# First query chunk of a causal attention turned to keys down the partitions, and the row statistics of chunks three and four moved ahead

## What is computed

```
xn = layernorm(x)
x_norm = (xn - mu) / sqrt(var + EPS) * gamma + beta
q, k, v = x_norm @ qkv[:, :512], x_norm @ qkv[:, 512:1024], x_norm @ qkv[:, 1024:]
scores = where(causal, (q @ k.T) / sqrt(512), -inf)
attn = softmax(scores) @ v @ o_proj + xn
h = silu(xn @ w_gate) * (xn @ w_up)
ffn = (of every 4 neighbours of h the 2 largest in size, the others 0) @ w_down
out = x + attn + ffn
```

## Time and profile before

| | us |
|---|---|
| median of 3 runs | 803.7 (800.33 to 805.3) |
| the profiled execution, its own time | 802.02 |
| span of the profile | 800.2 |
| PE busy | 788.8 (99%), 3518 matmuls |
| DVE busy | 610.8 (76%) |
| ACT busy | 319.6 (40%) |
| POOL busy | 18.9 (2%) |
| mean granted PE clock | 0.994 |

### The profile page before, as it was taken

How to read it: one execution, slowest core, us unless ns; L and a number is a source line. 1 busy time by engine, 2 the same in 40 slices (tenths; PEclk the granted TensorE clock), 3 DMA queues, 4 the chain that set the end, 5 groups by cost and what they waited for, 6 DMA issues and landing times.

```text
span 800.2 us, 9296 instructions
## 1 busy us (share of the span) xinstructions
PE 788.8 (99%) x3518; PEld 651.7 (81%) x3518; DVE 610.8 (76%) x964; ACT 319.6 (40%) x514; POOL 18.9 (2%) x26
## 2 busy tenths in 40 slices
PE   9999979989999999999999999999999999999998
PEld 6888858878888888888888888888888888888887
DVE  7978497775824688779989889799559558559786
ACT  5423142124312354564636436364334334335441
POOL 2010110101000000000000000000000000000000
PEclk9999989999999999999999999999999999999999
DMA  9441501730022325587426435497467262261002
GB/s 325 174 169 44 185 0 61 255 106 1 27 79 79 109 102 220 174 325 280 185 73 266 188 79 210 180 348 291 154 214 262 102 235 92 95 236 54 0 1 106
DMA packets 31611, 121.74 MB, mean 152 GB/s; under 512 B 3088, under 2 KB 3664, under 8 KB 29136
## 3 DMA queue, kind: packets, MB, share of 16 engines
q1 hardware_dynamic: 30272, 119.00, 40.4%
q10 hardware_dynamic: 1296, 2.16, 0.8%
HBM read 77.07 MB, written 44.07 MB: 151 GB/s over the span
## 4 chain that ended last, share of the span: by engine, by line
PE 78%; DMA 2%; DVE 1%; issue 0%; ACT 0%; SPq 0%; DVEq 0%
PE bank L960 13%; PE bank L961 13%; PE bank L962 13%; PE bank L1040 7%; PE bank L1042 7%; PE bank L1041 7%; PE bank L701 5%; PE bank L699 5%; PE bank L700 5%; PE bank L840 2%; DMA spread<-row_stats 1%; DMA resid<-rows 0%; DMA row_stats<-rows_turned_t 0%; DVE xh_raw L1541 0%; DVE xh_raw L1543 0%
## 5 line engine op out<-in xcount | busy, mean ns | idle before, releaser
L960 PE MATMUL bank<-X_hi,wset 128*128 128x512 f32 x448 | 174.4, 389 | 0.0
L962 PE MATMUL bank<-X_hi,wset 128*128 128x512 f32 x448 | 174.3, 389 | 0.0
L961 PE MATMUL bank<-X_lo,wset 128*128 128x512 f32 x448 | 174.3, 389 | 0.0
L960 PEld LDWEIGHTS bank<-X_hi,wset 128*128 128x128 f32 x448 | 84.1, 188 | 17.6 <-issue 0.2
L962 PEld LDWEIGHTS bank<-X_hi,wset 128*128 128x128 f32 x448 | 84.1, 188 | 17.5
L961 PEld LDWEIGHTS bank<-X_lo,wset 128*128 128x128 f32 x448 | 84.1, 188 | 17.4
L1040 PE MATMUL bank<-dw,hs_hi 128*128 128x512 f32 x224 | 87.2, 389 | 0.0
L1042 PE MATMUL bank<-dw,hs_lo 128*128 128x512 f32 x224 | 87.1, 389 | 0.0
L1041 PE MATMUL bank<-dw,hs_hi 128*128 128x512 f32 x224 | 87.1, 389 | 0.0
L1674 DVE TENSOR_TENSOR acc<-bank,acc 128x512 f32<-128x512 f32 x59 | 40.1, 687 | 40.0 <-PE bank L1042 39.6
L699 PE MATMUL bank<-zg,xT 128*128 128x512 f32 (+2 forms) x132 | 49.8, 377 | 0.0
(11 more groups left out here) (259 smaller groups left out, 1441.7 us busy)
## 6 DMA issues: line engine op xcount, KB each, us to landing
w_operands<-wset SPq DMA_DIRECT2D x8, 3584.0 KB, 13.5
wset<-w_operands SPq DMA_DIRECT2D x8, 3584.0 KB, 12.5
wsum<-w_units SPq DMA_DIRECT2D x28, 256.0 KB, 3.8
dw_raw<-L_ffn_w_down SPq DMA_DIRECT2D x14, 512.0 KB, 5.4
xw<-L_attn_x SPq DMA_DIRECT2D x4, 1024.0 KB, 9.6
xt_raw<-x_t SPq DMA_DIRECT2D x8, 512.0 KB, 7.5
xn_t<-xt_raw SPq DMA_DIRECT2D x8, 512.0 KB, 2.8
acc<-resid SPq DMA_DIRECT2D x2, 2048.0 KB, 9.8
```

Source lines behind the costliest of these rows:

```text
L960: pe.matmul(dst[:], u[:, 0, :], x_hi, start=(first and kt == 0), stop=False, skip_group_check=True)
L961: pe.matmul(dst[:], u[:, 0, :], x_lo, start=False, stop=False, skip_group_check=True)
L962: last = pe.matmul(dst[:], u[:, 1, :], x_hi, start=False, stop=(kt == 1), skip_group_check=True)
```

## The change

`WIDE` becomes all four chunks. The code of the other way (`scores`, `exp`, `head`, `attend`, with their turns, masks and buffers) goes away. Chunk 0 gets four units, a maximum with one half instead of two (`largest`), three softmax parts and its own sums (`first_sums`). All stores and loads of rows go to SP's queue. `turn_rows` puts the turned statistics of chunks 2 and 3 in bank 2 of the score ring (`LENT_BANK`), lent between two units of chunk 1. The statistics of chunk 2 move into chunk 0's softmax, those of chunk 3 amid the units of chunk 1. The core of the diff:

```
-    exp = [("exp", n, 0) for n in range(NT)]
-    WIDE = (1, 2, 3)
-    OLD = TC * WIDE[0]
-    for i in range(OLD):
-        ...
-        steps.append(("head", i, 0))
...
+    WIDE = range(NCH)
...
+    u = unit[0]
+    steps += [v[0][0], *u[0:2], x_scale[1], u[2], row_turn[1], row_copy[1], row_store[1], row_spread[1], u[3], ("max_all", 0, 0), v[0][1], *stat[2][0:2]]
+    steps += softmax(0, {-1: [v[0][2]], 0: [v[0][3]]}, {1: [*stat[2][2:4], x_stats[2], x_rstd[2]]})
+    steps += [xh_pre[1][0], *meet[0][0:2]]
+    steps += [step for k in range(KT) for step in (*xh_pre[1][k + 1:k + 2], xh[1][k], z_round[1][k])]
+    steps += [x_scale[2], meet[0][2], *z[1], ("sum_turn", 0, 0)]
     u = unit[1]
-    steps += [*u[0:2], ("rows_store", OLD - 1, 0), *stat[2], x_stats[2], x_rstd[2], xn[1][0], x_scale[2], xn[1][1], xn_store[1], xt_load[2], u[2],
...
+    steps += [u[0], row_turn[2], row_copy[2], row_store[2], row_spread[2], *rows_of[0][0], *rows_of[0][1], ("rows_load", 2, 0), ("rows_load", 3, 0),
+              u[1], *xn[1], xt_load[2], xn_store[1], *rows_of[0][2], *rows_of[0][3], ("rows_load", 4, 0), ("rows_load", 5, 0),
+              *stat[3], x_stats[3], x_rstd[3], xt_load[3], *u[2:4], x_scale[3], u[4], row_turn[3], row_copy[3], row_store[3], xh_pre[2][0], u[5],
+              xh_pre[2][1], xh[2][0], u[6], xh_pre[2][2], xh[2][1], u[7], ("max_fold", 1, 0), ("max_all", 1, 0),
+              xh_pre[2][3], xh[2][2], v[1][0], xh[2][3], *v[1][1:4], *z_round[2]]
...
-                if n == NCH - 1:
-                    pe.wait_ge(rows_ready, TC * (n - 1))
+                if n == 1:
+                    pe.wait_ge(prod_free, 2 * KT)
+                elif n == 3:
+                    pe.wait_ge(wide_kept, units_ahead[1] + LENT_BANK + 1)
                 pe.wait_ge(scale_ready, n + 1)
...
+                if c == 1 and u % PROD_RING == LENT_BANK:
+                    pe.wait_ge(turn_free, 2 + u // PROD_RING)
```

More of the change, by code:

```diff
@@ L77, in attention_ffn @@
     steps += [step for k in range(KT) for step in (*xh_pre[0][k + 1:k + 2], xh[0][k], z_round[0][k])]
[L78 to L84, removed]
-    WIDE = (1, 2, 3)
-    OLD = TC * WIDE[0]
-    for i in range(OLD):
-        steps += before.get(i, [])
-        steps.append(("head", i, 0))
[L91 to L96, removed]
+    steps += [*vo, *stat[1][0:2], *z[0], *stat[1][2:4], x_stats[1], x_rstd[1], xw_load[3]]
+    WIDE = range(NCH)
     def wide_units(c):
@@ L147, in attention_ffn @@
     steps += [("T4_load", 0, 0), *X_lo_steps[2:4], *X_hi_steps[5:], *X_lo_steps[4:], ("sum_turn", 3, 0), *rows_of[3][0], *rows_of[3][1], *rows_of[3][2], *rows_of[3][3]]
[L149 to L159, removed]
+    turn_no, prod_no, split_no = {}, {}, {}
     prods_before, turns_before = {}, {}
@@ L298, in small @@
             return at(name, o, [P, *cols], dt)
-        ident, causal, causal_t = small("ident", [P]), small("causal", [P]), small("causal_t", [P])
+        ident, causal_t = small("ident", [P]), small("causal_t", [P])
         gamma_t, beta_t = small("gamma_t", [KT]), small("beta_t", [KT])
@@ L735, in keys_of @@
                 return hi, lo
-            def score_product(n, g):
-                t, count = score_spans(n)[g]
-                no, a = prod_no["scores", n, g], n % TC * P
-                if n == 0:
-                    narrow(bank_of_product(no), [(*cols((zg_hi, zg_lo), q, 0, P), keys_both[:, :, q * W:q * W + P]) for q in range(KT)]).then_inc(prod_full, 1)
-                    return
-                dst = bank_of_product(no)[:, 0:count * P]
-                if t // TC != (t + count - 1) // TC:
-                    dst = dst.rearrange("p (b w) -> p b w", w=P)
-                three(dst, [(cols((zg_hi, zg_lo), q, a, a + P), keys_of(t, count, q)) for q in range(KT)]).then_inc(prod_full, 1)
-            def row_bank_free(no):
-                if no < TURN_RING:
-                    pe.wait_ge(prod_free, 2 * KT)
             def turn_rows(n):
@@ L1184, in _ @@
                     operands_hi(n, k)
-                elif kind == "rows_store" and n < OLD:
-                    act.wait_ge(rows_ready, n + 1)
-                    act.dma_start(resid_dram[n], rows[:, n % 2, :]).then_inc(resid_stored[n % 2], 16)
-                elif kind == "rows_load" and 2 <= n < OLD + 2:
-                    act.wait_ge(resid_stored[n % 2], 16 * (n // 2))
-                    act.dma_start(rows[:, n % 2, :], x_tiles[n]).then_inc(rows_loaded[n % 2], 16)
-                elif kind == "head":
-                    for g in range(len(key_tiles(n))):
-                        probs_hi(n, g)
-                elif kind == "exp":
-                    exponentials(n)
                 elif kind == "wide":
@@ L1447, in largest @@
                 dve.wait_ge(vec_step, masked)
-                wide_done[c] = step(nc.vector.tensor_tensor(half[:, u % 2, a:W], half[:, u % 2, a:W], block, ALU.max))
+                if c:
+                    wide_done[c] = step(nc.vector.tensor_tensor(half[:, u % 2, a:W], half[:, u % 2, a:W], block, ALU.max))
+                    return
+                one = max_one[0][:, a:W]
+                if u == 0:
+                    wide_done[c] = step(nc.vector.tensor_copy(one, block))
+                    return
+                dve.wait_ge(vec_step, wide_done[c])
+                largest_yet = nc.vector.tensor_tensor(one, one, block, ALU.max)
+                if u < TC - 1:
+                    wide_done[c] = step(largest_yet)
+                else:
+                    largest_yet.then_inc(max_folded, 1)
             def shift_part(c, j):
                 if j == 0:
-                    dve.wait_ge(max_reduced, c - WIDE[0] + 1)
+                    dve.wait_ge(max_reduced, c + 1)
                 units = wide_parts(c)[j]
@@ L1463, in shift_part, with first_sums @@
                 last.then_inc(shifted, 1)
+            def first_sums(j):
+                dve.wait_ge(exp_made, j + 1)
+                whole = sum_pair[0][:, 0, :]
+                if j == 0:
+                    sums_done[0] = step(nc.vector.tensor_copy(whole, raw_part(0, 0)))
+                    return
+                for u in wide_parts(0)[j]:
+                    some = whole[:, unit_cols(0, u):W]
+                    dve.wait_ge(vec_step, sums_done[0])
+                    added_up = nc.vector.tensor_tensor(some, some, raw_unit(0, u), ALU.add)
+                    if u < TC - 1:
+                        sums_done[0] = step(added_up)
+                    else:
+                        added_up.then_inc(sums_ready, 1)
             def add_part(c, j):
                 sums, units = sum_pair[c], wide_parts(c)[j]
+                if c == 0:
+                    first_sums(j)
+                    return
                 dve.wait_ge(exp_made, parts_ahead[c] + j + 1)
```

192 lines of the change are left out of this document (48 added, 144 removed).

## The result

The changed kernel takes 806.9 us (median of 14 runs, 804.8 to 807.6), the kernel before 802.5 on the same chip (14 runs, 800.3 to 805.3): ratio 1.0045, interval 1.003 to 1.0059. It is slower by 0.45%, and certainly so, but by less than the 1% that I had set as the bound of "no change". The profiled execution took 804.8, its span is 802.8 against 800.2 before. It is one of the shorter ones: ten of the 14 executions of the changed kernel are at 806 to 807.6, with a mean granted clock of 0.991 to 0.994 where this one has 0.996.

A forecast was written before the change was run, and what follows sets the result against it. PE, busy 99% of the span, was taken as the bound. Chunk 0's stage +4.4, its clock +1.0, chunk 1 +4.3 and chunk 2 -4.2 made +5.5 on 802.0: 807.5, stated as 808 us, range 797 to 816.

The forecast's parts named there:

- Chunk 0's stage: Chunk 0 up to chunk 1's first unit: waits of 0.5, 1.6 and 3.0 us, less 0.7 for fewer turns, 4.4 us longer.
- The clock there: In chunk 0: a PE wait of 3.0 us may bring the granted clock down, put in at 1.0 us.
- POOL's change of code: Before chunk 0's all-reduce: POOL changes code in 8.7 us, 0.2 showing; rival, longer, at its bound of 20 giving 816, chance 0.07.
- The turn of chunk 3: After five units of chunk 1: PE waits 9.7 us for chunk 3's statistics, with ends of 5.6 and 12.
- The store held by the spread: SP's queue in chunk 1: row store behind the 1 MB spread lands at 91.3, rows at 94.0, 3.2 us lost.
- the 0.8 for POOL beside DVE: At chunk 3's statistics: POOL and DVE lock each other out on SBUF; without that rule the sum is 0.8 us less.
- The last `v` ahead of `z`: End of chunk 1's units: last `v` product directly ahead of `z_round`, its bank free 1.4 us later, 0.8 lost.
- The clock: In chunk 1: the granted clock surely falls after the long wait for chunk 3's statistics, put in at 2.5 us.
- Chunk 2's units: Chunk 2, with chunk 3's statistics and spread done earlier: the old wait of 2.4 and clock loss of 1.8 go, -4.2 us.

## Why the prediction was right

The time was 806.9 for 808.0 predicted, within 1% as I held likeliest. By its steps:

- **Chunk 0's stage, +4.4.** It measured +4.2: 0.44, 1.30 and 2.75 of wait (4.5) for 0.5, 1.6 and 3.0 (5.1), while the turns that went saved 0.3 and not 0.7. Chunk 1's first unit stands at 80.23 for 80.1. The clock there, 1.0, is absent from the profiled execution. It is there in the run that kept POOL and DVE apart: a fall of 3.4 us, worth 1.7.
- **POOL's change of code** was mis-sized. I took 8.7 us from a row at the program's start; the all-reduce began at 51.12, 0.1 after the maximum was folded and 6.8 after the last power, so a change of code took at most 6.8. It added nothing that the profile shows, as DVE was busy anyway. The Trainium skill, GPSIMD Engine Reference, section 2.1 Instruction dispatch, gives about 6 us for the first call after fresh code; the trace leaves room for that and not for the 8.7 of my row, whose idle time at the program's start must have been something more or something else. It shows no lower bound.
- **The turn of chunk 3, 9.7 us.** It measured 9.05, and each link held: rows of tile 2 at 94.08 for 94.0, statistics at 99.55 for 99.5, POOL 3.25 for 3.5, turn at 103.33 for 103.5. The store held by the spread, which no row had shown, is confirmed by the run that parted them (3.1 us), the 0.8 for POOL beside DVE by the run that parted those (0.9). The Trainium skill, SBUF — State Buffer, section "SBUF: two separate sides", was the reason to expect the latter; the trace agrees, for POOL's step of 1.11 ended at 100.75, 0.1 after DVE's pass over 1024 columns, and took 0.23 without it.
- **The last `v` ahead of `z`**: 0.72 for 0.8. My reason was wrong: this product stood directly ahead of `z_round` before as well, and the 0.72 is what is left there of the 5.0. **The clock**: one fall of 6.8 us from 99.49, of which PE had work in some 3, so it cost 1.5 for 2.5 put in.
- **Chunk 2's units, -4.2**: -4.6, the wait and the clock's fall both gone.

In the profiled executions the sum is then +2.8 (804.8 against 802.0), where I had +5.5: 2.0 of the difference is clock, 0.7 the turn's wait. But the profiled execution is the exception. The run that kept POOL and DVE apart has the falls that I had put in: 3.4 us in chunk 0 (1.7) and 10.2 us from 99.2 at the turn, of which PE had work in 4.9 (2.5), together 4.2 for my 3.5. Its mean clock of 0.992 is that of most executions of the changed kernel, so these probably have the same falls; none of them was profiled. That the time was hit to 1.1 us owes something to luck all the same, since the errors of 0.4 and more in single terms have both signs. That the waits were hit does not.

What I did not see was how far the cause lies in one place. I priced the form of chunk 0 at its own stage, +4.4, and the waits of chunk 1 as the price of the early statistics. The runs say the opposite: the form costs some 9 us, over half of it in chunk 1, most likely since it moves chunk 0's rows onto DVE's late stretch, and the early statistics of chunk 2 repair 5.4 of it. What stays open is why some executions have a fall of the clock in chunk 0 and others none.

## What to carry to other kernels

When a change of order takes one stall away, follow the list of the engine that was late, not the step that was waited for: here DVE's list from the first rows to the low parts of `v` set the pace, so moving the turn 16 us further gave 3 us but left 6.7 of its 9.1 us of wait, and the next places turned what was left into waits on `v_lo` or at a meet. Edits that gave DVE a late input earlier, or work later, gained besides, and three together came to 9 us. Once DVE's own list is no longer the late one, as behind the load of `xt_raw`, shortening it gives nothing. A step that another engine must read and copy back (a turn, then a copy) has two ends; a place that is free for the one can be a stall for the other. Before a large broadcast is put into a queue, look at which small stores and loads are needed soon behind it.

## What the runs showed of the hardware

- A store behind a spread of 1 MB in the same queue: the load that waits for it went out 6.2 us after it (85.42 to 91.58), and 2.0 us after it (86.01 to 88.03) with the spread behind.
- A small instruction of POOL (128x4) took 1.11 us beside a pass of DVE over 128x1024 of 1.19 us, and 0.23 with DVE idle.
- POOL's all-reduce began 6.8 us after a plain instruction (44.29 to 51.12), 0.1 us after its input was there: a change of code between the two, if there is one, fits into 6.8 us.
- A wait of TensorE of 1.3 us ahead of the first meet left the clock full in each profile that has it. One of 8 to 9 us had a fall of 6.8 or 10.2 us in each, which began while TensorE still waited (at 99.5 in a wait from 94.3 to 103.3). One of 2.7 us had a fall of 3.4 us in five of six. A fall costs only where TensorE has work: 3 of 6.8 us in the changed kernel.
